# Moving the shift between the result and the weights' copy in VectorE's expert slot, and scaling four slots ahead

## The reference

```
x = normalised tokens; aff = x @ centroids.T; assign = argmax(aff)      # 8 experts, one per token
xn = layernorm(x) * ln_g[e] + ln_b[e]
h  = relu(xn @ w1[e].T + b1[e])                                        # 512 hidden
y  = x + h @ w2[e].T + b2[e];  a = sigmoid(x . centroid[e])
out = a * y + (1 - a) * x                                              # = x + a * b2[e] + a * (h @ w2[e].T)
```

## Time and profile before

| what | value |
|---|---|
| median of 3 runs | 360.68 us (358.99 to 361.7) |
| the profiled execution's own time | 359.23 us |
| its span in the profile | 357.5 us |
| PE busy | 338.0 us, 95% |
| DVE busy | 285.2 us, 80% |
| POOL busy | 250.4 us, 70% |
| ACT busy | 241.0 us, 67% |

### The profile page before, as it was taken

How to read it: one execution, slowest core, us unless ns; L and a number is a source line. 1 busy time by engine, 2 the same in 40 slices (tenths; PEclk the granted TensorE clock), 3 DMA queues, 4 the chain that set the end, 5 groups by cost and what they waited for, 6 DMA issues and landing times.

```text
span 357.5 us, 17464 instructions
## 1 busy us (share of the span) xinstructions
PE 338.0 (95%) x6868; PEld 292.3 (82%) x6868; DVE 285.2 (80%) x786; ACT 241.0 (67%) x657; POOL 250.4 (70%) x244
## 2 busy tenths in 40 slices
PE   7899999999999999999999999999999999999980
PEld 7567777777766877877787889999999999999970
DVE  8898798798887799987897768788787778878850
ACT  4897858858756756765766547666766766776650
POOL 3388659889986875554656206888888888788884
PEclk9999999999999999999999999999999999999995
DMA  6413231222223233255332326455555455453420
GB/s 196 107 30 88 68 93 31 85 79 72 85 77 85 93 106 118 89 145 158 100 101 79 93 57 120 69 77 65 71 73 73 64 74 77 64 75 46 38 23 0
DMA packets 46705, 28.99 MB, mean 81 GB/s; under 512 B 5096, under 2 KB 44320, under 8 KB 46624
## 3 DMA queue, kind: packets, MB, share of 16 engines
q1 hardware_dynamic: 34352, 19.34, 19.7%
q0 software_dynamic: 12272, 8.54, 16.9%
HBM read 14.53 MB, written 13.78 MB: 79 GB/s over the span
## 4 chain that ended last, share of the span: by engine, by line
PE 66%; DVE 11%; issue 8%; POOL 5%; ACT 2%; POOLq 1%; DVEq 0%; ACTq 0%
PE bank L1480 13%; PE sc L1472 13%; PE sc L1317 8%; PE bank L1370 7%; POOL out_dram L507 5%; DVE pr L880 4%; PE bank L1379 4%; PE bank L1243 3%; PE bank L1252 3%; PE bank L1265 2%; PE bank L1337 2%; PE sc L1465 2%; PE bank L1298 2%; PE bank L1258 2%; PE bank L1348 1%
## 5 line engine op out<-in xcount | busy, mean ns | idle before, releaser
L507 POOL DMA_INDIRECT out_dram<-qx,rows x71 | 114.1, 1606 | 40.1 <-issue 21.3
L715 ACT ACTIVATE qx<-sc,b1T 128x128 f32<-128x128 f32 x280 | 79.8, 368 | 39.1 <-PE sc L1472 39.0
L427 POOL DMA_INDIRECT slots_d<-rows,pos_i x64 | 62.4, 975 | 34.5 <-issue 8.6
L1480 PE MATMUL bank<-tokens,qx 128*128 128x128 f32 x568 | 75.3, 276 | 0.4 <-ACT qx L715 0.4
L1472 PE MATMUL sc<-wide,tokens 128*128 128x128 f32 x560 | 74.0, 275 | 0.0
L880 DVE TENSOR_TENSOR pr<-sc,causal 128x1536 f32<-128x1536 f32 (+2 forms) x33 | 63.5, 1923 | 8.2 <-PE sc L1317 6.6
L1480 PEld LDWEIGHTS bank<-tokens,qx 128*128 128x128 f32 x568 | 69.1, 192 | 0.7 <-ACT qx L715 0.6
L1472 PEld LDWEIGHTS sc<-wide,tokens 128*128 128x128 f32 x560 | 68.2, 192 | 0.0
L1042 DVE COPY tokens<-xT 128x1024 f32 x71 | 55.6, 784 | 0.2 <-issue 0.2
L1057 DVE SCALAR_TENSOR_TENSOR qx<-bank,rows,qx 128x128 f32<-128x128 f32 x71 | 24.9, 350 | 25.0 <-PE bank L1480 24.3
L550 ACT ACTIVATE qx<-bank,gmask 128x512 f32<-128x512 f32 x64 | 41.1, 686 | 4.1 <-PE bank L1243 4.1
(11 more groups left out here) (167 smaller groups left out, 520.9 us busy)
## 6 DMA issues: line engine op xcount, KB each, us to landing
rows<-slots_d SPq DMA_DIRECT2D x71, 66.0 KB, 2.0
out_dram<-tokens SPq DMA_DIRECT2D x16, 256.0 KB
tokens<-in_L_attn_x_dram SPq DMA_DIRECT2D x7, 512.0 KB, 4.6
w1raw<-in_L_ffn_w_dram SPq DMA_DIRECT2D x8, 256.0 KB, 2.9
w2raw<-in_L_ffn_w_dram SPq DMA_DIRECT2D x8, 256.0 KB, 2.7
out_dram<-qx,rows POOLq DMA_INDIRECT x71, 3.3
slots_d<-rows,pos_i POOLq DMA_INDIRECT x64, 2.8
slots_d<-empty SPq DMA_DIRECT2D x9, 66.0 KB
```

Source lines behind the costliest of these rows:

```text
L427: pool.indirect_dma_start(slots_d, bass.IndirectOffsetOnAxis(ap=pos_i[:, t:t + 1], axis=0), rows[:, t, :], None)\
L507: pool.indirect_dma_start(out_rows, bass.IndirectOffsetOnAxis(ap=xs[:, a, D + 2:D + 3].bitcast(U32), axis=0), ye[:, a, :], None, bounds_ch ...
L715: last = nc.scalar.activation(ht[:, k % 2, c * P:(c + 1) * P], inner(k)[:, c * P:(c + 1) * P], ACT.Relu, bias=b1T[:, bass.ds(e * FC + c, 1)])
L1480: last = mm(banks[k % 2][:, 0:D], ht[:, k % 2, c * P:(c + 1) * P], ws[:, k % 3, F + c * D:F + (c + 1) * D], start=(c == 0), stop=(c == FC ...
```

## The change

In VectorE's slot k the result of slot k - 1 now comes first, then the shift of slot k, then the copy of the weights of slot k + 2, and last the scaling of slot k + 4. The scaling of slot 3 is done ahead of the loop. No instruction is added or taken away, and no wait or buffer is changed.

```diff
             se_scale(2)
             result(NQ - 1)
+            se_scale(3)
 
             dve.wait_ge(s("sc_ps"), NH)
...
                     k = RING * i + a
-                    if k + 3 < NS:
-                        se_scale(k + 3)
-                    se_shift(k, e[a + 2])
                     if k > 0:
                         se_result(k - 1)
+                    se_shift(k, e[a + 2])
                     if k + 2 < NS:
                         se_weights(k + 2, e[a + 4])
+                    if k + 4 < NS:
+                        se_scale(k + 4)
             se_result(NS - 1)
```

## The result

The changed kernel takes 361.04 us (median of 15 runs, 359.95 to 362.56), the kernel before 359.33 us (15 runs). The ratio is 1.0043, 95% interval 1.0029 to 1.0058: slower by 0.4%, 1.7 us. The profiled execution took 361.03 us with a span of 359.3 us, against 359.23 and 357.5.

A forecast was written before the change was run, and what follows sets the result against it. TensorE was taken to set the pace at 1.90 us a slot, with GpSimd as full. Moves cost zero; the later copy 41 x 0.045 = 1.8 us, added to the median 360.68: 362.5 us, range 359.2 to 365.2.

The forecast's parts named there:

- the 41 slots: Expert-stage slots, of 70, counted in locked stretches; each to cost 0.045 us, 1.8 us in all.
- the median of three runs: Base time of the kernel before, 360.68 us, to which the forecast added 1.8 us.
- the lock: GpSimd's instructions and VectorE's weights' copies keep step; TensorE would follow GpSimd's held 1.94 us, costing 0.045 us a slot.
- The scaling and the register load at zero: VectorE's moved scaling, and the register load now behind it at ring starts, were each to cost zero.
- nothing in itself: VectorE's shift, moved behind the result, was to cost nothing itself, as the result needing it comes a slot later.
- the upper bound: If GpSimd's single delays do not break the lock, all 70 slots cost 0.045 us: 3.1 us.
- The single delays: Delays of GpSimd, as at 266.65 and 310.60 us, that moved the copy's phase elsewhere outside the locked stretches.
- rival B: GpSimd ends sooner, with TensorE not late: end up to 1.9 us sooner, 359.1 us; chance 0.12.
- Rival A: No lock at the later time, TensorE not late, only a lag of +0.3 us: 361.0 us; chance 0.22.
- Rival C: VectorE bounds at ring starts, TensorE late by 0.38 us at each of eight: 365.5 us; chance 0.16.
- The sign that I named for the lateness: TensorE's first weight load of L1472 would show idle time ended by VectorE's L1042, some 1.5 to 2 us together.
- The rule weighed: Skill's rule that a VectorE copy and GpSimd instruction block each other wholly; change worth nothing, 360.7 us.

The follow-up runs named there:

- the shift alone: Against the kernel before, only the shift moved between the result and the weights' copy, the scaling staying at the slot's start: 361.10 us, ratio 1.005.
- the pair without GpSimd's DMAs: Order before and changed order, each with GpSimd adding only the last slot to the output: 358.41 and 358.21 us, against 359.55 for the kernel before.
- second shift: Changed kernel plus a second copy of the shift, written to an unread place just ahead of the real one: 361.02 us, 1.005 of the kernel before.
- a copy a slot further ahead: Changed kernel with four weight buffers and the copy of slot k + 3 in slot k: 357.86 us, 0.9948 of the kernel before.
- register load moved: Kernel before with its cyclic order kept, but the ring-start register load between shift and result instead of between copy and scaling: 359.41 us, ratio 0.9999.

## Why the prediction was right or wrong, point by point

- **The step that failed** is "With the 41 slots: 41 x 0.045 = 1.8 us, both at TensorE's end and at GpSimd's last start". Both halves of it are wrong. It was not 41 slots but practically all: the results took 3.0 us longer (135.3 against 132.3). And GpSimd's last start did not follow TensorE's end: its lag fell from 3.61 to 1.78 us, a term of -1.8 us that the sum put at nothing. A third number that the time rests on, the median of three runs, was 1.35 us too high (below).
- **The mechanism of the lock held.** The copy starts one shift later; a held copy ends 1.55 us into GpSimd's instruction; TensorE's weight load is late by 0.10 us (1.62 us behind the result); the pair settles where the slot is GpSimd's held 1.94 us, with the copy 0.575 us into the instruction by the prediction and 0.54 to 0.57 measured. The scaling and the register load at zero were right for the changed kernel (the shift alone gives the same time), and so was "nothing in itself" for the shift (the pair without GpSimd's DMAs).
- **That 1.8 us forecast met 1.7 us measured is luck.** The step took the locked stretches of before as they were. The 3.0 us at TensorE are the 3.1 us that I had set as the upper bound. The single delays that broke the lock before did not come, or were overrun: at the 50th instruction there is 0.30 us of idle time instead of 0.86, and no instruction of 2.01 or 2.06 us.
- **What I had as rival B was a part of the outcome.** The lag at the end did fall by 1.8 us, of the 1.9 us that B priced, though TensorE was late all the time, which B was to exclude. I treated B as a separate case where it was a term of the same sum: at TensorE +3.0, at the lag -1.8, so +1.1 us for the stage. The profiled pair shows 1.8 because its first result also came 0.67 us later (216.0 against 215.3). The two profiles of before differ there by 1.1 us, so this may be chance. The medians differ by 1.7 us; the 0.6 us between this and the stage's 1.1 us is not explained by the profiles.
- **The time itself, 362.5 us, is 1.5 us too high**, because I added 1.8 us to a median of three runs, 360.68. Fifteen runs put the kernel before at 359.33, close to its profiled 359.23, so the profiled time was the better base; 359.23 + 1.8 = 361.0 us is what came. Within 1%, which I gave 0.78, is where it ended, but as a loss that 15 runs tell from zero: I had said that 1% is about what can be told, and the interval is 0.3% wide.
- **Rival A** (no lock, only the lag) had named 361.0 us, which is the measured time, but it is out by the 1.94 us slots. Its premise, that the late weight load might be free, fails: the load came 0.10 us later than before and the slots grew. **Rival C** (VectorE binds at ring starts) is out: results still waited 0.21 to 0.24 us for TensorE at the ring starts.
- **The sign that I named for the lateness was wrong in form.** No idle time stands before L1473. It shows as a longer mean of the matmuls and as a smaller wait of the result. The mean copy, put at 0.86 us, came to 0.954, which is the same miss as the 41 slots.
- **The rule weighed** (the Trainium skill, SBUF — State Buffer, "Who interferes with whom": whoever issues first blocks the other for the whole instruction) does not describe these rows. Copies of 0.68 us ran unstretched within GpSimd's instruction wherever they ended before 1.2 us into it, and a copy 0.24 us into it cost nothing. The trace agrees only in that copy and instruction do hold each other up, at the places listed below. By the rule the change would have been worth nothing.

## What to carry to other kernels

When two engines run at nearly the same period and hold each other up at one place in it, look at their relative phase, not at their busy shares: plot the start of the one within the instruction of the other. Here a delay of 0.27 us on an engine with slack cost nothing as long as no third engine waited for what was held; once TensorE did, the held pace became that of every slot, and a further 0.26 us of delay left the median where it was. A slot of reserve (a fourth buffer) took the cost away with the copy still in the bad place; the better place in the order did as well. When you change one such pair, ask also where the other engine ends: the lag at the end was worth as much as the lock. Compare stages by their own lengths, since starts vary more than the effect.

## What the runs showed of the hardware that was not expected

- GpSimd's indirect DMA of 1.56 us and VectorE's weights' copy of 0.68 us disturb each other at two places. The first is about 1.2 us into the instruction. A copy in progress there that would end sooner is held until 1.55 us, and the instruction takes 1.64 us. A copy that would end later keeps its 0.68 us, and the instruction ends 0.08 to 0.09 us behind it: 1.76 us for a copy that starts 0.99 us into it (second shift), 1.81 for 1.04 (a copy a slot further ahead), 2.06 for 1.29 (before).
- The second place is the instruction's start. A copy that would end about there is stretched to 0.18 us into the instruction and makes it 1.60 to 1.61 us. A copy that began 0.11 us ahead of the start kept its 0.68 us, and the instruction took 2.01 us (in three profiles).
- A scaling (0.28 us) that started about 0.50 us into GpSimd's instruction with a copy behind it mostly took 0.55 to 0.62 us, and the instruction then 1.70 to 1.71, though copies that ran over the same stretch alone were not held. One scaling of 0.59 us without a copy behind it, at 319.2 us in the kernel before, stood in an instruction of 1.61 us like its neighbours.
- The phase pattern came back within a few hundredths of a microsecond in the two profiles of the kernel before and in the one with the register load moved, the single disturbances at the 50th and the 56th instruction included.
